# Chunk row sums spread by DMA instead of TensorE, one product one column narrower, and a last chunk finished tile by tile

## What is computed

```
e   = layernorm(x) @ a1 + (in2 @ a2).T          # s1 (one per row) + s2 (one per column)
e   = where(e > 0, e, 0.2 * e)
att = softmax(where(adj > 0, e, -9e15), axis=1) * adj.sum(1, keepdims=True)
x   = x + (0.1 * att + 0.9 * adj) @ in2
out = x + layernorm(x) @ weight.T + bias
```

## Time and profile before

| what | us |
|---|---|
| median of three runs (394.04 to 394.32) | 394.11 |
| the profiled execution's own time | 394.79 |
| its span, first to last instruction | 393.0 |
| PE busy | 367.2 |
| DVE busy | 311.6 |
| ACT busy | 250.6 |
| POOL busy | 128.2 |

### The profile page before, as it was taken

One profiled execution on the slowest core, in us unless ns is written; L12 is line 12 of the kernel. 1 busy time (PEld: TensorE's weight loads), 2 busy tenths in 40 slices (PEclk: granted clock), 3 DMA queues, 4 the chain that ended last, 5 costly groups with the idle time before them and its releaser, 6 DMA issues.

```text
span 393.0 us, 8864 instructions
## 1 busy us (share of the span) xinstructions
PE 367.2 (93%) x3237; PEld 319.4 (81%) x3237; DVE 311.6 (79%) x790; ACT 250.6 (64%) x638; POOL 128.2 (33%) x255
## 2 busy tenths in 40 slices
PE   0398999999999999999999999999999999999991
PEld 0277888888888888888888888888888888888881
DVE  3989889989995977959596886959598695959873
ACT  2797998797685673919376491928558291946100
POOL 1697141516250605033150604215060412400101
PEclk9999999999999999999999999999999999999996
DMA  7999997566674572909265381917447000000000
GB/s 200 242 213 214 220 186 161 109 135 124 145 139 103 103 154 44 211 17 175 67 128 131 66 189 18 196 56 140 104 88 169 15 13 15 3 1 15 15 0 30
DMA packets 17357, 42.81 MB, mean 109 GB/s; under 512 B 1936, under 2 KB 8608, under 8 KB 17312
## 3 DMA queue, kind: packets, MB, share of 16 engines
q0 software_dynamic: 9216, 33.56, 44.1%
q1 hardware_dynamic: 8096, 8.67, 7.0%
HBM read 73.66 MB, written 2.11 MB: 193 GB/s over the span
## 4 chain that ended last, share of the span: by engine, by line
PE 89%; DMA 7%; POOL 2%; DVE 1%; issue 0%; SPq 0%; POOLq 0%; ACT 0%; DVEq 0%
PE acc_u L599 29%; PE acc_v L599 29%; PE acc_y L599 26%; DMA adj_all<-adj 5%; PE small L593 2%; PE small L579 2%; DMA x_pre<-x 1%; PE turned L568 1%; POOL adj_all L334 1%; POOL pre_rstd L344 0%; POOLq L43 0%; POOL post_rstd L377 0%; DVE pre_st L739 0%; SPq L274 0%; DVE late L842 0%
## 5 line engine op out<-in xcount | busy, mean ns | idle before, releaser
L449 ACT ACTIVATE steep<-s_bc,steep_s 128x256 bf16<-128x256 f32 x512 | 208.0, 497 | 11.6 <-DVE plus L757 9.9
L599 PE MATMUL acc_y<-weights_y,adj_all 128*128 128x258 f16 x1024 | 121.9, 275 | 3.1 <-DMA adj_all<-adj 2.1
L599 PE MATMUL acc_v<-weights_v,minus 128*128 128x258 f16 x1024 | 120.3, 273 | 0.0
L599 PE MATMUL acc_u<-weights_u,plus 128*128 128x258 f16 x1024 | 120.3, 273 | 0.0
L599 PEld LDWEIGHTS acc_y<-weights_y,adj_all 128*128 128x128 bf16 x1024 | 100.2, 98 | 19.7 <-DMA adj_all<-adj 2.0
L599 PEld LDWEIGHTS acc_u<-weights_u,plus 128*128 128x128 bf16 x1024 | 99.7, 97 | 14.7
L599 PEld LDWEIGHTS acc_v<-weights_v,minus 128*128 128x128 bf16 x1024 | 99.8, 98 | 14.4
L757 DVE TENSOR_TENSOR plus<-adj_all,steep 128x2048 bf16<-128x2048 bf16 x64 | 78.5, 1227 | 2.5 <-ACT steep L449 2.5
L760 DVE TENSOR_TENSOR minus<-adj_all,plus 128x2048 bf16<-128x2048 bf16 x64 | 78.4, 1226 | 2.2
L462 ACT ACTIVATE num<-acc_u,ac 128x129 f32<-128x129 f32 x32 | 11.5, 363 | 104.8 <-PE acc_u L599 104.8
L374 POOL TENSOR_SCALAR post_var<-post_mv 128x2 f32<-128x2 f32 x16 | 3.4, 215 | 161.9 <-DVE post_mv L821 161.9
(11 more groups left out here) (78 smaller groups left out, 250.4 us busy)
## 6 DMA issues: line engine op xcount, KB each, us to landing
adj_all<-adj POOLq DMA_DIRECT2D x64, 512.0 KB, 9.4
plus<-in SPq DMA_DIRECT2D x4, 512.0 KB, 7.1
x_pre<-x SPq DMA_DIRECT2D x16, 128.0 KB, 6.2
x_res<-x SPq DMA_DIRECT2D x16, 128.0 KB, 6.3
out<-late SPq DMA_DIRECT2D x16, 128.0 KB, 1.7
s_rows<-s_bc SPq DMA_DIRECT2D x16, 1.0 KB
steep<-a SPq DMA_DIRECT2D x1, 64.0 KB, 3.4
a_bc<-a SPq DMA_DIRECT2D x1, 64.0 KB, 5.5
```

Source lines behind the costliest of these rows:

```text
L449: ins = nc.scalar.activation(steep[:, h, k, :], s1_bc[b][:, :], ACT.Relu, bias=steep_s2[:, jt:jt + 1], scale=STEEP)
L599: ins = nc.tensor.matmul(acc[:, 0:2 * WC], left[:, jt, cols(t)], right[:, jt, :, :].rearrange("p a b -> p (a b)"), start=(jt == 0), stop=( ...
```

## The change

Three edits are made together.

**s1 by DMA.** From chunk 5 on (`SPREAD = 5`) PE no longer spreads s1 and ACT no longer copies it. SP waits for `pre_s1`, stores its 256 values, one element at a time, to the chunk's row in DRAM, waits for that store and for the sign tests of the chunk that used the buffer before, and loads the row back into all 128 partitions of `s1_bc`. ACT's sign tests wait for that load.

**Y narrower.** The Y product takes 257 of the 258 columns, and the zero column is no longer written.

**Last chunk.** The slot of the last chunk has an order of its own. PE transposes chunk 14 before U of tile 1, does the linear part of chunk 14 before V of tile 1, and transposes tile 0 of chunk 15 between the third and the last quarter of that V. After it come the linear part of tile 0, the transpose of tile 1 and its linear part. DVE, ACT, POOL and SP follow tile by tile, so that moments, normalization, copy, product, final add and store handle 128 columns each. The four quarters of `range_check` move to slots 10 to 13, one in each.

```diff
             def store_s1(n, b):
-                sp.wait_ge(s1_ready, n + 1)
-                sp.dma_start(s1_rows[n:n + 1, :], s1_bc[b][0:1, :]).then_inc(s1_stored[b], 16)
+                if n < SPREAD:
+                    sp.wait_ge(s1_ready, n + 1)
+                    sp.dma_start(s1_rows[n:n + 1, :], s1_bc[b][0:1, :]).then_inc(s1_stored[b], 16)
+                else:
+                    sp.wait_ge(pre_pool, PRE * n + 3)
+                    sp.dma_start(s1_rows[n].rearrange("(t p) -> p t", p=P), pre_s1[b][:, :],
+                                 allow_slow_non_contiguous=True).then_inc(s1_stored[b], 16)
+                    sp.wait_ge(s1_stored[b], landed(n, b))
+                    sp.wait_ge(steep_done, 4 * n - 4)
+                    sp.dma_start(s1_bc[b][:, :], s1_rows[n].partition_broadcast(P)).then_inc(s1_landed[b], 16)
...
-                        if q == 0:
+                        if q == 0 and c + 1 < SPREAD:
                             act.wait_ge(s1_ready, c + 2)
+                        elif q == 0:
+                            act.wait_ge(s1_landed[1 - b], s1_in(c + 1, 1 - b))
                         sign_tests(c + 1, q, 1 - b)
...
-                        if ahead(c, 2):
+                        if c + 2 < SPREAD:
                             copy_spread(c + 2, b)
...
-                            if ahead(c, 2):
+                            if c + 2 < SPREAD:
                                 spread(c + 2, b)
...
-                    ins = quarter(acc_y[t], adj_b[f], w_y, t, q)
+                    ins = quarter(acc_y[t], adj_b[f], w_y, t, q, WC + D)
...
+                if not ahead(c, 1):
+                    pe.wait_ge(tile_left, 2 * c - 1)
+                    product(acc_u[0], plus[b], w_u, 0, plus_ready, c).then_inc(u_done, 1)
+                    product(acc_v[0], minus[b], w_v, 0, minus_ready, c).then_inc(tile_done, 1)
+                    turn(c - 1)
+                    pe.wait_ge(tile_left, 2 * c)
+                    product(acc_u[1], plus[b], w_u, 1, plus_ready, c).then_inc(u_done, 1)
+                    linear(c - 1)
+                    for q in range(QUARTERS - 1):
+                        quarter(acc_v[1], minus[b], w_v, 1, q)
+                    turn_tile(0)
+                    quarter(acc_v[1], minus[b], w_v, 1, QUARTERS - 1).then_inc(tile_done, 1)
+                    return
...
-            turn(CHUNKS - 1)
-            linear(CHUNKS - 1)
+            linear_tile(0)
+            turn_tile(1)
+            linear_tile(1)
...
-                if c == CHUNKS - 1:
-                    for q in range(QUARTERS):
-                        range_check(q)
+                if c >= RANGE_AT - QUARTERS and c < RANGE_AT:
+                    range_check(c - RANGE_AT + QUARTERS)
+                if not ahead(c, 1):
+                    epilogue(c, 0, b)
+                    last_moments(c, 0)
+                    last_normal(c, 0, b)
+                    finish(c - 1, 1 - b)
+                    epilogue(c, 1, b)
+                    last_moments(c, 1)
+                    last_finish(c, 0, b)
+                    last_normal(c, 1, b)
+                    last_finish(c, 1, b)
+                    return
...
+            last_rstd(last, 0)
+            pool.wait_ge(out_ready, last)
+            last_bias(last, 0, last % 2)
+            last_bias(last, 1, last % 2)
+            last_rstd(last, 1)
```

More of the change, by code:

```diff
@@ L39 @@
 GEN = 31
+SPREAD = 5
 def gnn_ffn(nc, x, adj, in2, a1, a2, w_t, bias, s1_rows, out):
@@ L165, in gnn_ffn @@
         s1_ready = sem("s1_ready")
+        s1_landed = [sem(f"s1_landed{b}") for b in range(2)]
         consts_ready = sem("consts_ready")
@@ L238, in landed, with s1_in @@
             return 16 * (n // 2 + 1)
+        def s1_in(n, b):
+            return 16 * ((n - b) // 2 - (SPREAD - b + 1) // 2 + 1)
         def adj_in(n, f):
@@ L303, in _ @@
             last = (CHUNKS - 1) % 2
-            sp.wait_ge(out_ready, CHUNKS)
-            sp.dma_start(out[CHUNKS - 1], o_buf[last]).then_inc(out_stored[last], 16)
+            for t in range(TILES):
+                sp.wait_ge(out_ready, CHUNKS + t)
+                sp.dma_start(out[CHUNKS - 1][:, cols(t)], o_buf[last][:, cols(t)]).then_inc(out_stored[last], 16)
             count = range_left(sp)
             for b in range(2):
-                sp.wait_ge(out_stored[b], 16 * CHUNKS // 2)
+                sp.wait_ge(out_stored[b], 16 * CHUNKS // 2 + (16 if b == last else 0))
             for b in range(2):
@@ L349, in row_sums @@
                     pool.wait_ge(ac_ready, n - 1)
-                    pool.wait_ge(s1_spread, n - 1)
+                    pool.wait_ge(s1_spread, min(n - 1, SPREAD))
+                    if n - 2 >= SPREAD:
+                        pool.wait_ge(s1_stored[b], landed(n, b) - 16)
                 nc.gpsimd.tensor_tensor(pre_s1[b][:, :], pre_dot[b][:, :], pre_rstd[b][:, :],
@@ L534, in slot @@
                     [0, 1, "first", "second", "copies", 2, 3] if c == 1 else \
-                    [0, 1, "first", 2, 3, "second", "copies"]
+                    [0, 1, "first", 2, 3, "second", "copies"] if ahead(c, 1) else \
+                    ["first", "copies", "second"]
                 for step in order:
                     if step == "copies":
-                        if ahead(c, 2):
+                        if c + 2 < SPREAD:
                             copy_spread(c + 2, b)
@@ L551, in _ @@
             run_slots(slot)
-            copy_turned(CHUNKS - 1)
+            for t in range(TILES):
+                act.wait_ge(xn_turned, CHUNKS + t)
+                if t == 0:
+                    act.wait_ge(ffn_done, CHUNKS - 1)
+                nc.scalar.activation(xn_t[:, cols(t)], xnt_ps[:, cols(t)], ACT.Copy).then_inc(xnt_ready, 1)
             with act.If(range_left(act) != 0):
@@ L595, in linear, with quarter @@
                 ins.then_inc(ffn_done, 1)
-            def quarter(acc, left, right, t, q):
+            def quarter(acc, left, right, t, q, width=2 * WC):
                 for jt in range(q * QJ, (q + 1) * QJ):
-                    ins = nc.tensor.matmul(acc[:, 0:2 * WC], left[:, jt, cols(t)],
-                                           right[:, jt, :, :].rearrange("p a b -> p (a b)"),
+                    ins = nc.tensor.matmul(acc[:, 0:width], left[:, jt, cols(t)],
+                                           right[:, jt, :, :].rearrange("p a b -> p (a b)")[:, 0:width],
                                            start=(jt == 0), stop=(jt == JT - 1))
@@ L632, in y_quarter @@
                 for t in range(TILES):
-                    ins = quarter(acc_y[t], adj_b[n], w_y, t, q)
+                    ins = quarter(acc_y[t], adj_b[n], w_y, t, q, WC + D)
                     if q == QUARTERS - 1:
@@ L697, in slot, with turn_tile, linear_tile @@
                     y_product(c + 2, 1, (f + 2) % BUFS)
+            def turn_tile(t):
+                pe.wait_ge(xn_ready, CHUNKS + t)
+                if t == 0:
+                    pe.wait_ge(xnt_ready, CHUNKS - 1)
+                nc.tensor.transpose(xnt_ps[:, cols(t)], xn[:, t, :], ident[:, :]).then_inc(xn_turned, 1)
+            def linear_tile(t):
+                pe.wait_ge(xnt_ready, CHUNKS + t)
+                if t == 0:
+                    pe.wait_ge(out_ready, CHUNKS - 1)
+                nc.tensor.matmul(ffn_ps[:, cols(t)], xn_t[:, cols(t)], wt_sb[:, :],
+                                 start=True, stop=True).then_inc(ffn_done, 1)
             run_slots(slot)
-            turn(CHUNKS - 1)
-            linear(CHUNKS - 1)
+            linear_tile(0)
+            turn_tile(1)
+            linear_tile(1)
             with pe.If(range_left(pe) != 0):
@@ L982, in slot, with last_moments, last_normal, last_finish @@
                 post_start(c)
-                if not ahead(c, 1):
-                    finish(c - 1, 1 - b)
+            def last_moments(n, t):
+                if t == 0:
+                    wait_apart(dve, post_pool, 2 * n)
+                wait_apart(dve, tile_left, 2 * n + t + 1)
+                nc.vector.bn_aggr(post_mv[:, t, :], post_st[:, t, :]).then_inc(post_moments, 1)
+            def last_normal(n, t, b):
+                dve.wait_ge(post_pool, 2 * n + 2 * t + 2)
+                dve.wait_ge(post_moments, 2 * n + t + 1)
+                if t == 0:
+                    dve.wait_ge(xn_turned, n)
+                nc.vector.tensor_scalar(xn[:, t, :], x1[b][:, t, :], post_mv[:, t, 0:1],
+                                        post_rstd[:, t:t + 1], ALU.subtract, ALU.mult).then_inc(xn_ready, 1)
+            def last_finish(n, t, b):
+                dve.wait_ge(ffn_done, n + t + 1)
+                dve.wait_ge(x1b_ready, n + t + 1)
+                if t == 0:
+                    dve.wait_ge(out_stored[b], 16 * (n // 2))
+                nc.vector.tensor_tensor(o_buf[b][:, cols(t)], ffn_ps[:, cols(t)], x1_bias[:, t, :],
+                                        ALU.add).then_inc(out_ready, 1)
             run_slots(slot)
```

(3 more changed lines are left out.)

16 lines of the change are left out of this document (13 added, 3 removed).

## The result

The changed kernel takes 388.94 us (median of 4 runs, 388.77 to 389.29) against 394.22 us for the kernel before in the same comparison: 5.3 us less, a ratio of 0.987 with a 95% interval of 0.984 to 0.989. The forecast was 388.1 us, with a range of 387.2 to 389.8.

A forecast was written before the change was run, and what follows sets the result against it. PE's instruction list was taken to bound the kernel. Savings of 4.92 us (spreads), 0.2 (column) and 0.87 (last chunk) summed to 6.0 us, taking the 394.11 us median to 388.1 us, range 387.2 to 389.8.

The forecast's parts named there:

- What bounds the kernel: Dense stretch: the 22.58 us slot is PE's instruction list and nothing else; DVE at 17.4 us is the next bound.
- Part 1: Slots 3 to 13: 11 spreads of 0.447 us leave PE's list, 4.92 us less, the DMA transfers costing nothing.
- my upper bound of 16.9: Longest s1 round trip by DMA: store 10.7 us plus load 6.2 us, with elements taking turns with big packets.
- The 11 us that I took: Expected s1 round trip: the store starts before the DMA engines fill, the load ends inside the burst.
- The limit of 27 us: Slots with s1 by DMA: s1 must land within 27 us of being ready, counted back from the last mask quarter.
- s1 comes too late: Rival, chance 0.03: s1 lands past the limit, each us beyond costing 11; at 30 us the time is 421 us.
- Part 2: Y groups whose time PE's list sets: one column less in 896 matmuls saves 0.2 us, between 0 and 0.4.
- The equal pitch of the two rows I weighed: PE matmuls: 258-column Y at 111.8 ns and 128-column float32 passes at 112 ns may mean a floor, giving nothing.
- Part 3: Last chunk and tail: -1.43 us after the last product, +0.56 ahead of it, net -0.87, between -0.4 and -1.6.
- the tail gives nothing back: Rival at the end, chance 0.10: a transpose stall or slow store eats the 0.87 us or twice that; 389.0 us.
- The new transpose: Last slot, before V's last quarter: tile 0 ready at 11.7 us, PE there at 14.1; cover 2.4 us, no stall.
- The range checks and new waits in the slots: Slots 10 to 13: range checks fit DVE's 4.7 us free per slot and cost nothing; new waits might cause stalls.

The follow-up runs named there:

- e1: Kernel before with only the spreads of chunks 5 to 15 moved to DMA, old widths and old last slot: 389.58 us, ratio 0.989 to before.
- e9: Kernel before with s1 also stored element by element from chunk 5 on, PE still spreading and no row loaded: 394.09 us, one run.
- e8: Changed kernel with the store of s1 made twice, one after the other, before the load: 460.15 us, ratio 1.166 to before.
- e7: Changed kernel with 226 columns in 31 of the 32 matmuls of each Y group: 378.44 us, one run.
- e2: Kernel before with only the Y product narrowed to 257 columns: 394.04 us, ratio 0.999 to before.
- e6: Changed kernel with 256 columns in 31 of the 32 matmuls of each Y group: 389.08 us, one run.
- e3: Changed kernel with every spread on PE and Y at 258 columns, leaving the last chunk's order and moved range checks: 393.99 us, ratio 0.999 to before.
- e5: Changed kernel without the branch for unusual inputs and the reads of its flag, range checks kept: 388.32 us, ratio 0.986 to before.
- e4: Changed kernel with one last store of 128 KB in place of two of 64 KB: 389.35 us, ratio 0.988 to before.
- e12: Changed kernel with chunk 14's linear part after the last product, s1 by DMA from chunk 4, stored in 8-byte runs: 390.87 us, ratio 0.991 to before.
- e10: Changed kernel with chunk 14's linear part and range matmul after the last product, POOL's deviations before its bias adds: 388.72 us, ratio 0.986 to before.

## Why the prediction was right, point by point

By the traces the change is worth 4.05 us in A, 2.04 in B and -0.76 in C, 5.3 in all, and the medians say 5.3. I had said 6.0. The number fell into the range because the largest term was right; the smaller ones were off in both directions and partly cancelled. By its own steps:

- **What bounds the kernel: right.** PE's list set every slot, before and after.
- **Part 1, 4.92 us: right,** 4.91 alone (e1). That the trip costs nothing was right too, but its size was wrong: 17.6 us, over my upper bound of 16.9. Of the two terms of that bound the store kept to its own, 8.9 us where I had 10.7, and the load did not, 8.7 where I had 6.2: I took the row's time from a trace without element stores, and with them such loads take longer (`x_pre` 9.9 us). The 11 us that I took failed on the store too. I had counted on it starting before the engines fill, but it takes almost as long without any burst: the one issued at 329.15 us in the changed kernel, when no `adj` load is left, landed in 7.5 us. That the stores would slow other transfers (e9) the prediction does not have at all; it cost nothing here, since their readers are a slot or more away.
- **The limit of 27 us: wrong.** I counted back from the mask that PE needs, and left out what stands behind the sign tests in ACT's list, the copy of the transposed rows, which PE's linear part needs ahead of Y and of DVE's next statistics. That is a ring of two slots, which leaves 21.4 to 22.5 us for the trip by my estimates (e8). The rival "s1 comes too late" was some 4 us away, not 9, and in e7, whose slots are shorter, it came true for one slot; its chance of 0.03 rested on the 9. Its price was wrong too: by the ring, a us beyond the limit costs 5.5 us over 11 slots at the dense clock, not 11, and PE's slower clock comes on top.
- **Part 2, 0.2 us: wrong in size,** 0 (e2). The equal pitch of the two rows I weighed did not come from a floor that binds float16 matmuls, since 226 columns go below it (e7); 257 columns cost what 258 do all the same, and 256 less (e6).
- **Part 3, 0.87 us: too large.** Ahead of the last product I counted +0.56 and it was +0.87: the range matmul, which sits inside the linear part of chunk 14, came along (0.12 us), and the linear part took 0.64 us behind it, not 0.45. Behind it, I counted -1.43 and B gave -2.04, 0.4 us of it from a clock that had not yet fallen (transpose 0.34 us where I took 0.47, linear part 0.49 where I took 0.78). That was luck: e3 and e5 have the same order at the end, and their linear part took 0.78 and 0.81 us. C took 0.76 back, for which I had 0 to -0.3: the rival "the tail gives nothing back", by a mechanism that I had not named (e4, e5). Together the part gave 0.4 us here, and alone it shows 0.1 us (e3). The new transpose did not stall, as forecast: tile 0 was normalized at 373.34 us and PE came to it at 376.65, a cover of 3.3 us.
- **The range checks and new waits in the slots: right,** no cost.

## What to carry to other kernels

Where one engine's list fills the time, the gain of taking an instruction off it is its length times its count, and can be forecast to the hundredth; the rest of the work is to find the ring that closes through what replaces it. Count that ring over as many slots as it spans, all engines' order included: slack counted to one consumer alone was some 5 us too generous here. And read the ring's length at the clock that the kernel runs at: a ring measured while PE stalls is longer than it would be in the dense kernel (24.7 against 21.8 us). And a small transfer hidden from its own reader can still be costly for others: count its elements, not its bytes.

## What the runs showed of the hardware

- A store of 256 elements of 4 bytes takes 7.5 to 8.1 us with quiet DMA engines and 8.6 to 10.8 beside the loads in the changed kernel, and up to 19.2 once in e7; one of 128 runs of 8 bytes 2.6 to 3.7 (e12).
- Such a store slows large loads issued at the same moment: 512 KB from 9.4 to 15 us (e9).
- Matmuls of 258 and 257 float16 columns both have a pitch of 111.8 ns (e2); 256 columns 1.5 ns less (e6), 226 columns 15.1 ns less (e7).
- A last store of 64 KB whose packets a fetch of instructions falls among took 3.1 and 3.2 us (changed kernel, e3), against 1.5 without one (e5).
- PE's granted clock was still 1.00 when tile 1's linear part ran in the changed kernel, after 3.8 us of quiet, a transpose of 0.33 us and 0.4 us of quiet again. In e3 and e5, with the same order, it was down to 0.55 and 0.50 at that piece. In the old end it was 0.50 from 386.97 us on, after 3.9 us of quiet, and in e10 it was 0.50 after 2.4 us of quiet, 0.46 us of work and 0.5 us of quiet. The same two passes took 0.49 or 0.79 us from one kernel to the next, so a term of some tenths in such a tail can't be forecast.
